# Graph attention on one core: a prologue written out chunk by chunk, and the adjacency turned into a bias by another engine

## The chip, the cores and the metric

One core of a Trainium2 chip runs the whole kernel. The metric is the device time of one execution in microseconds, the median over several runs. TensorE (PE) multiplies matrices, VectorE (DVE) and ScalarE (ACT) read its results out of PSUM, GpSimd (POOL) works in SBUF only, and SyncE (SP) issues DMAs. POOL and SP each issue DMAs into a queue of their own.

## The reference

Cut to what matters (N = 4096 rows, 256 features, 8 heads of 64):

```
h = max(layernorm(x), 0)
adj = max(adjacency, eye)
q, k, v = h @ Wq[head], h @ Wk[head], h @ Wv[head]
scores = q @ k.T / 8 + 0.01 * eye - 1e16 * (1 - adj)
out = x + sum over heads of softmax(scores) @ v @ Wo[head]
```

The adjacency is a float 4096 x 4096 matrix of zeros and ones.

## The kernel before, in words

The eight heads go in two groups of four. Each group has its own programs for the five engines, written one after the other: a prologue that makes keys K2 (a high and a low part, for accuracy) and values V for all 4096 rows, and then 64 steps, one for each head of each pair of row tiles (16 pairs of 256 query rows, four heads). The two groups are called group 0 and group 1 below. The order of work of each engine is written by hand, with semaphores between the engines.

**Prologue.** The rows go in NC = 8 chunks of 512. In group 0, DVE takes the statistics of a chunk of x (`bn_stats`, L647, L650, L652), POOL raises the variance to the power -0.5 (L319), DVE normalises (L658), PE transposes (L393), ACT takes the maximum with zero into `hc` and writes it to a DRAM scratch hT (L557, L560). Group 1 reads hT back (L178) from SP's queue. Then PE makes keys (L407) and values (L422), ACT and DVE read them out of PSUM (L566, L671 for keys, L572, L677 for values). The chunks run in a loop with two buffers, each chunk's values right behind its keys. After the last chunk, PE makes the first head's score slots (L449) with nothing between them.

**A step.** A score row of 4096 columns is cut in SPT = 4 slots of 1024; a step has SLOTS = 8 slots (two row tiles q = 0, 1, four slots k each). For slot j, PE makes the scores into `psS[j % 2]` (L449) and DVE's `mask` adds the bias tile B and takes the row maximum in one instruction (L702). ACT takes the exponential (L589). For the last 16 of the 32 key tiles ("late" ones) DVE transposes blocks of 32 x 32 (L723, twice a step, once for each q) and 32 DMAs of 64 KB put the blocks in place, 16 issued by SP (L248) and 16 by POOL (L307), eight for each q. PE transposes the other key tiles (L462, ACT copies them out, L596) and multiplies with V (L472, and L486 for the late tiles). The masks run one head ahead: step h masks slots 2 to 7 of head h+1 and slots 0 and 1 of head h+2. `mask` of slots 4 to 7 writes where the late blocks of the head before were staged, so it waits for the moves of that head: slots 4, 5 for the two halves of q = 0, slots 6, 7 for those of q = 1. L623 is ACT's copy of the odd half of a step's output, the last instruction of a step on ACT; its start is taken as the end of the step.

**The bias.** B holds (adj - 1) * 1e16 * 8 in bf16 for one pair of row tiles, for all four heads. In group 0, POOL loads it from the adjacency with a cast (L287, eight DMAs a pair) and turns it into the bias itself (`convert`, L293, eight a pair); the diagonal is cleared with `notI` (L298) in the one slot `own_slot` that holds the pair's own columns. The own slot is 0 for pairs 0 to 3, 1 for pairs 4 to 7, 2 for 8 to 11, 3 for 12 to 15. Group 0 also stores the finished bias to DRAM (`keep_bias`), and group 1 loads it back from SP's queue (L184) with no conversion. For pair i+1 this is done in steps h = 2 and h = 3 of pair i, when the last head's masks free B slot by slot. POOL's order in step 2 is: moves of q = 0, loads 0 and 1, moves of q = 1, loads 2 and 3, the base rows (L310), then

```
for half_ in range(2):
    for k in (2 * half_, 2 * half_ + 1):
        convert(i + 1, 0, k, own_slot)
    for k in (2 * half_, 2 * half_ + 1):
        load_adj(i + 1, 1, k)
for k in range(2):
    convert(i + 1, 1, k, own_slot)
```

and in step 3 the moves of both q, then the last two conversions.

Of the kernel before, what the change touches and what calls it, by code (L numbers as in the profile page):

```python
# [6 lines left out]
ACT = mybir.ActivationFunctionType  # L7
# [31 lines left out]
NC = N // CH  # L39
EPS = 1e-5  # L40
# [41 lines left out]
def group_programs(nc, sem, g, before, x, hT, adj, bias, Wk, Wq, Wv, Wo, base, result, t):  # L82
# [5 lines left out]
    (K2, V, S, B, PT, QH, QL, hq, wq, wo, O, Oodd, RB, acc, res, ident, notI, diag, mx, negm, sums, den, rden,  # L88
# [8 lines left out]
    x_in = [sem(f"x_in{g}{b}") for b in range(2)]  # L97
    h_in = [sem(f"h_in{g}{b}") for b in range(2)]
    h_out = [sem(f"h_out{g}{b}") for b in range(2)]
    (w_in, wqo_in, half_set, stat1, aggr, var_ready, rstd_ready, normed, x_transposed, h_ready, k_proj, v_proj, k_hi, k_lo,  # L100
     v_act, v_dve) = (sem(f"{s}{g}") for s in (
         "w_in", "wqo_in", "half_set", "stat1", "aggr", "var_ready", "rstd_ready", "normed", "x_transposed", "h_ready",
# [9 lines left out]
    (bias_conv, bias_ready, q_proj, q_hi, q_lo, scores_ready, slot_masked, row_ready, probs_ready,  # L112
# [3 lines left out]
            "bias_conv", "bias_ready", "q_proj", "q_hi", "q_lo", "scores_ready", "slot_masked", "row_ready",  # L116
# [3 lines left out]

    def chunks(engine, body):

        with engine.Fori(0, NC // 2 - 1) as i:
            for b in range(2):
                body(i, b, True, True)
        body(NC // 2 - 1, 0, True, False)
        body(NC // 2 - 1, 1, False, False)

    def after(i, b):

        return (i, 1) if b == 0 else (i + 1, 0)

    def query_psum(first):

        return psT[0] if first else psP
# [31 lines left out]
    if not norm:  # L167
        late_used_before, late_moved_before, late_sent_before, slot_masked_before, projected_before, o_summed_before, head_added_before, bias_kept_before = before

    def sync_program(sp):  # L170
# [3 lines left out]
        def load_x(i, b):  # L174
            sp.dma_start(xb[b], x_v[bass.ds(i * 2 + b, 1), :, :, :].rearrange("a p r d -> p (a r) d")).then_inc(x_in[b], 16)

        def load_h(i, b):
            sp.dma_start(hc[b], hT[:, :, bass.ds((i * 2 + b) * CH, CH)]).then_inc(h_in[b], 16)  # L178


# [16 lines left out]
        load = load_x if norm else load_h  # L197
        if not norm:
            sp.wait_ge(late_used_before, STEPS - 1)
        load(0, 0)  # L200
        if not norm:
            for q in range(QT):
                for half in range(HALVES):
                    sp.wait_ge(late_moved_before[q][half], MOVED * STEPS)
                    sp.wait_ge(late_sent_before[q][half], MOVED * STEPS)
        for w, dst in ((Wk, wk), (Wv, wv)):
            for c in range(DC):
                sp.dma_start(dst[:, c, :].rearrange("p (h k) -> p h k", k=KD),
                             w[heads, c * P:(c + 1) * P, :].rearrange("h p k -> p h k")).then_inc(w_in, 16)
        load(0, 1)  # L210
        if not norm:
            sp.wait_ge(projected_before, STEPS + START)
        for c in range(DC):
            sp.dma_start(wq[:, c, :].rearrange("p (h k) -> p h k", k=KD),
                         Wq[heads, c * P:(c + 1) * P, :].rearrange("h p k -> p h k")).then_inc(wqo_in, 16)
        Wo_v = Wo[heads, :, :].rearrange("(a e) k d -> e k a d", e=2)
        for e in range(2):
            sp.dma_start(wo[e * KD:(e + 1) * KD, :, :], Wo_v[e]).then_inc(wqo_in, 16)
        if not norm:
# [5 lines left out]
        with sp.Fori(0, NC // 2 - 1) as i:  # L225
            for b in range(2):
                if norm:
                    sp.wait_ge(x_transposed, i * 2 + b + 1)
                else:
                    sp.wait_ge(v_proj, i * 4 + (2 * b + 2 + START))  # L230
                load(i + 1, b)


        if norm:
            sp.wait_ge(h_out[0], 16 * (1 + START))
        load_hq(0)
        if norm:
            for b in range(2):
                sp.wait_ge(h_out[b], 16 * (NC // 2 + START))
# [39 lines left out]
    def gpsimd_program(pool):  # L279
# [9 lines left out]
        def convert(i, q, k, own_slot):  # L289

            wait_apart(pool, adj_in[q][k], i * 16 + 16, pool_passed)
            part = B[:, q, k * SLOT:(k + 1) * SLOT]
            done = nc.gpsimd.tensor_scalar(part, part, -1.0, MASK_VAL / SCALE, ALU.add, ALU.mult)  # L293
            if k == own_slot:
                done.then_inc(bias_conv, 1)
                pool.wait_ge(bias_conv, i * QT + q + 1)
                own = B[:, q, bass.ds(i * QW + q * P, P)]
                done = nc.gpsimd.tensor_tensor(own, own, notI[:, :], ALU.mult)  # L298
            done.then_inc(bias_ready, 1)
# [16 lines left out]
        def inverse_deviation(i, b):  # L316

            pool.wait_ge(var_ready, i * 2 + (b + 1))
            nc.gpsimd.tensor_tensor(rstd[:, b, :], mv[:, b, :, 1], half[:, :], ALU.pow).then_inc(rstd_ready, 1)  # L319

# [594 lines left out]
```

## Time and profile before

| what | value |
|---|---|
| median of 3 runs | 2713.36 us (2710.54 to 2719.93) |
| the profiled execution's own time | 2709.6 us |
| its span, first to last instruction | 2708.1 us |
| mean granted TensorE clock | 0.994 |
| busy share: PE, DVE, ACT, POOL | 97%, 83%, 68%, 47% |
| first score matmul of group 0, of group 1 | 85.51 us, 1439.23 us |
| first PE transpose of step 0, group 0 and group 1 | 101.10 us, 1454.64 us |

A row of a timeline has start and duration in us, the engine, the line of the kernel, the operation, output<-inputs, the shape and the number of instructions merged (x); in brackets stands how long the engine sat idle before it, and what released it. A row of a waits view has the waiting instruction, what it waited for, the total in us, how many times, and the longest. A row of a windows view has the stretch, its length, and busy time of each engine with instruction counts, then the granted clock, the share of the DMA engines that was busy, and GB/s. A row on one instruction has min/median/max of its duration in ns. PE counts as busy while a matmul is in its pipeline.

### The profile page before, as it was taken

The page shows a single profiled execution, that of the slowest core. Times are in us where ns is not written, and L with a number is a line of the kernel's source. Part 1 is how long each engine was busy: PE and PEld are TensorE (multiplying, and loading weights), DVE is VectorE, ACT ScalarE, POOL GpSimd, SP SyncE. Part 2 cuts the span into 40 slices and gives each one's busy share as a digit, 9 for nine tenths or more (in the row PEclk, how much of TensorE's full clock was granted, in tenths as well). Part 3 has the DMA queues.
Part 4 walks back from the last instruction along what each step waited for, and adds up shares of the span by engine and source line. Part 5 has one row for each costly group of instructions (what it writes and reads, how often), then busy time and mean ns, then how long its engine had stood idle before and what let it go on. Part 6 is the DMA issues. An engine that isn't in the chain of part 4 may idle for free. (4 is left out here: it accounts for less than half of the span.)

```text
span 2708.1 us, 58752 instructions
## 1 busy us (share of the span) xinstructions
PE 2630.7 (97%) x17344; PEld 1901.9 (70%) x17344; DVE 2253.6 (83%) x3833; ACT 1850.8 (68%) x3041; POOL 1280.6 (47%) x2418
## 2 busy tenths in 40 slices
PE   7899999999999999999998999999999999999997
PEld 5666777767777776766766777777777777777775
DVE  6788888888888888888847888888888888888885
ACT  3576777767767676776745777777777777777774
POOL 2356655566565556655512444444444444343433
PEclk9999999999999999999999999999999999999999
DMA  6367766677776677776652566656565656555654
GB/s 163 111 143 177 184 163 175 165 168 167 173 190 170 164 177 166 171 171 169 167 142 76 146 158 151 158 142 145 138 151 145 164 146 162 133 146 138 157 144 106
DMA packets 263358, 418.51 MB, mean 155 GB/s; under 512 B 98944, under 2 KB 119936, under 8 KB 259200
## 3 DMA queue, kind: packets, MB, share of 16 engines
q1 hardware_dynamic: 172032, 228.88, 33.0%
q0 software_dynamic: 89088, 184.69, 29.7%
q10 hardware_dynamic: 2176, 4.19, 0.4%
q8 instruction: 28, 0.46, 0.1%
q14 instruction: 34, 0.28, 0.0%
HBM read 136.31 MB, written 46.27 MB: 67 GB/s over the span
## 5 line engine op out<-in xcount | busy, mean ns | idle before, releaser
L307 POOL DMA_DIRECT2D S<-S x2048 | 1007.8, 500 | 1137.1 <-DVE S L723 1089.6
L702 DVE CUSTOM_DVE_ANT_0 S<-psS,B 128x1024 f32<-128x1024 f32 x1024 | 1228.4, 1218 | 268.3 <-PE psS L449 155.1
L589 ACT ACTIVATE S<-S,negm 128x1024 f32<-128x1024 f32 (+1 forms) x768 | 1095.8, 1428 | 88.8 <-DVE negm L709 88.3
L596 ACT ACTIVATE PT<-psT 128x512 f32<-128x512 f32 x1024 | 595.0, 596 | 267.5 <-PE psT L462 248.5
L449 PE MATMUL psS<-K,QH 128*128 128x512 f32 x2048 | 729.2, 437 | 35.7 <-DVE mx L702 31.5
L449 PE MATMUL psS<-K,QL 128*128 128x512 f32 x2048 | 642.5, 395 | 0.0
L462 PEld LDWEIGHTS psT<-ident,S 128*128 128x128 f32 x4096 | 481.2, 140 | 192.0 <-issue 73.5
L462 PE MATMUL psT<-ident,S 128*128 128x128 f32 x4096 | 608.0, 276 | 7.8 <-ACT S L589 4.9
L723 DVE STREAM_TRANSPOSE S<-S 128x2048 f32<-128x2048 f32 x256 | 590.2, 2306 | 27.6 <-PE psO L486 23.7
L472 PE MATMUL psO<-PT,V 128*64 128x256 f32 x4096 | 492.1, 382 | 0.0
L486 PE MATMUL psO<-S,V 128*64 128x256 f32 x4096 | 470.3, 382 | 2.0 <-DMA S<-S 2.0
L449 PEld LDWEIGHTS psS<-K,QL 128*128 128x128 f32 x2048 | 385.3, 188 | 87.4
L486 PEld LDWEIGHTS psO<-S,V 128*64 128x64 f32 x4096 | 283.6, 137 | 176.5 <-issue 48.0
L472 PEld LDWEIGHTS psO<-PT,V 128*64 128x64 f32 x4096 | 283.4, 137 | 175.0 <-ACT PT L596 23.7
L449 PEld LDWEIGHTS psS<-K,QH 128*128 128x128 f32 x2048 | 313.6, 191 | 82.0 <-DVE mx L702 69.6
L623 ACT ACTIVATE Oodd<-psO 64x256 f32<-64x256 f32 x128 | 48.9, 382 | 400.7 <-PE psO L472 400.7
L293 POOL TENSOR_SCALAR B<-B 128x1024 bf16<-128x1024 bf16 x128 | 133.4, 1052 | 59.6 <-DMA B<-in_adj 58.4
L589 ACT ACTIVATION_READ_ACCUMULATOR S<-S,negm 128x1 f32 x768 | 146.0, 190 | 0.0
L685 DVE TENSOR_TENSOR QL<-psP,QH 64x256 fp32r<-64x256 f32 x248 | 104.4, 421 | 3.6
L708 DVE TENSOR_TENSOR S<-S,diag 128x128 f32 (+1 forms) x256 | 75.2, 294 | 30.9 <-DVE mx L702 23.3
L580 ACT ACTIVATE QH<-psP 64x256 fp32r<-64x256 f32 x248 | 93.1, 375 | 2.2
L702 DVE DVE_READ_ACCUMULATOR2_ANT mx<- 128x1 f32 x1024 | 84.9, 83 | 0.0
(51 smaller groups left out, 967.9 us busy)
## 6 DMA issues: line engine op xcount, KB each, us to landing
S<-S SPq DMA_DIRECT2D x2048, 64.0 KB, 3.1
S<-S POOLq DMA_DIRECT2D x2048, 64.0 KB, 2.9
B<-in_adj POOLq DMA_DIRECT2D x128, 256.0 KB, 7.2
bias_scratch<-B SPq DMA_DIRECT2D x32, 1024.0 KB, 5.8
B<-bias_scratch SPq DMA_DIRECT2D x128, 256.0 KB, 5.1
hq<-hT_scratch SPq DMA_DIRECT2D x32, 256.0 KB, 3.5
RB<-rden_scratch SPq DMA_DIRECT2D x128, 64.0 KB, 3.2
S<-in_x SPq DMA_DIRECT2D x8, 512.0 KB, 3.6
```

The costliest lines, as they stand in the source:

```text
L293: done = nc.gpsimd.tensor_scalar(part, part, -1.0, MASK_VAL / SCALE, ALU.add, ALU.mult)
L307: pool.dma_start(dst, src).then_inc(late_sent[q][half], 16)
L449: last = nc.tensor.matmul(psS[j % 2][:, b * BANK:(b + 1) * BANK], part[:, h, q * P:(q + 1) * P], K2[:, h, col:col + BANK], start=hi, stop= ...
L462: last = nc.tensor.transpose(psT[s % 2][:, a * QW + q * P:a * QW + (q + 1) * P], S[:, h % 2, q, col:col + P], ident[:, :])
L472: last = nc.tensor.matmul(psO[a * KD:(a + 1) * KD, 0:QW], V[:, 2 * s + a, h * KD:(h + 1) * KD], PT[:, s % RING, a * QW:(a + 1) * QW], star ...
L486: last = nc.tensor.matmul(psO[half_ * KD:(half_ + 1) * KD, 0:QW], V[:, MT - LATE + m, h * KD:(h + 1) * KD], PTL[:, m, :, :, :], start=Fals ...
L580: last = nc.scalar.activation(QH[half_ * KD:(half_ + 1) * KD, h + e, :], query_psum(first)[e * KD:(e + 1) * KD, 0:QW], ACT.Copy)
L589: nc.scalar.activation(part, part, ACT.Exp, bias=negm[:, h % 2, q:q + 1], accum_out=sums[:, h % 2, q, e:e + 1]).then_inc(probs_ready, 1)
L596: nc.scalar.activation(PT[:, s % RING, :], psT[s % 2][:, :], ACT.Copy).then_inc(pt_act, 1)
L685: last = nc.vector.tensor_tensor(QL[rows, h + e, :], query_psum(first)[e * KD:(e + 1) * KD, 0:QW], QH.bitcast(F32)[rows, h + e, :], ALU.su ...
L702: nc.vector.tensor_tensor_reduce(out=part, in0=psS[j % 2][:, :], in1=B[:, q, k * SLOT:(k + 1) * SLOT], scale=SCALE, scalar=LOWEST, op0=ALU ...
L723: nc.vector.transpose(dst, src).then_inc(late_transposed, 1)
```

## The change

- **Prologue, written out.** Instead of a loop over two buffers there are four x buffers (XB = 4) and a buffer of `hc` for every chunk (chunks 0 to 3 in S of even heads, 4 to 7 in S of odd heads). PE makes keys of all chunks in order; values of chunks 0 to 3 (EARLY = 4) go between the keys, one chunk behind; values of chunks 4 to 7 go amid the first head's score slots, one chunk behind each two slots. wv moves into a buffer of PT. The first query goes to `psP` and is made after the keys of chunk 6. The normalisation goes from DVE to POOL, the stores of hT from ACT's queue to SP's.
- **Group 1's start.** SP issues the loads of h chunks 0 to 3, wq and hq first, then Wk, then Wv, then chunks 4 to 7. Group 0's last projection is made by PE behind the keys of group 1's chunk 0.
- **The bias.** POOL no longer converts. `add_self` clears the diagonal of the adjacency block (`notI`) and adds the identity (`eye`), two instructions of 128 columns. DVE converts each slot right before it masks it, in place, and waits for its own conversion.

```diff
-        def convert(i, q, k, own_slot):
-            wait_apart(pool, adj_in[q][k], i * 16 + 16, pool_passed)
-            part = B[:, q, k * SLOT:(k + 1) * SLOT]
-            done = nc.gpsimd.tensor_scalar(part, part, -1.0, MASK_VAL / SCALE, ALU.add, ALU.mult)
...
+        def add_self(i, q, own_slot):
+            wait_apart(pool, adj_in[q][own_slot], i * 16 + 16, pool_passed)
+            own = B[:, q, bass.ds(i * QW + q * P, P)]
+            nc.gpsimd.tensor_tensor(own, own, notI[:, :], ALU.mult).then_inc(self_cleared, 1)
+            wait_apart(pool, self_cleared, i * QT + (q + 1), pool_passed)
+            nc.gpsimd.tensor_tensor(own, own, eye[:, :], ALU.add).then_inc(self_added, 1)
...
         def step(i, h, more, prev, own_slot):
             move_late(i, h, 0)
-            if adj_step:
-                for k in range(2):
-                    load_adj(i + 1, 0, k)
+            if adj_rest:
+                add_self(i + 1, 1, own_slot)
             move_late(i, h, 1)
...
+            if adj_step:
+                for k in range(SPT):
+                    load_adj(i + 1, 0, k)
             if prev and h == 2:
                 pool.wait_ge(stored, i * 16)
                 load_base(i)
             if adj_step:
...
+                add_self(i + 1, 0, own_slot)
+                for k in range(SPT):
+                    load_adj(i + 1, 1, k)
...
         def mask(i, h, j, first=False):
             if h == 0 and norm:
+                dve.wait_ge(self_added, i * QT + (q + 1))
+                wait_apart(dve, adj_in[q][k], i * 16 + 16, dve_passed)
+                part = B[:, q, k * SLOT:(k + 1) * SLOT]
+                nc.vector.tensor_scalar(part, part, -1.0, MASK_VAL / SCALE, ALU.add, ALU.mult).then_inc(bias_ready, 1)
                 dve.wait_ge(bias_ready, i * SLOTS + (j + 1))
...
         def rows_again():
             sp.wait_ge(late_used_before, STEPS - 1)
+            for n in range(EARLY):
+                load_h(n)
+            load_weights(Wq, wq, wq_in)
+            load_hq(0)
             for q in range(QT):
                 for half in range(HALVES):
                     sp.wait_ge(late_moved_before[q][half], MOVED * STEPS)
                     sp.wait_ge(late_sent_before[q][half], MOVED * STEPS)
+            load_weights(Wk, wk, w_in)
+            sp.wait_ge(late_used_before, STEPS)
+            sp.wait_ge(pt_free_before, RING + STEPS * TS)
+            load_weights(Wv, wv, wv_in)
+            for n in range(EARLY, NC):
+                load_h(n)
...
+        def normalise(n):
+            pool.wait_ge(var_ready, n + 1)
+            b = n % XB
             nc.gpsimd.tensor_tensor(rstd[:, b, :], mv[:, b, :, 1], half[:, :], ALU.pow).then_inc(rstd_ready, 1)
+            pool.wait_ge(rstd_ready, n + 1)
+            for r in range(CR):
+                last = nc.gpsimd.tensor_scalar(xb[b][:, r, :], xb[b][:, r, :], mv[:, b, r, 0:1], rstd[:, b, r:r + 1],
+                                               ALU.subtract, ALU.mult)
+            last.then_inc(normed, 1)
...
+        for n in range(NC):
+            keys(n)
+            if n == 0 and not norm:
+                project_before(pe)
+            if norm and n + 2 < NC:
+                transpose_x(n + 2)
+            if 0 < n <= EARLY:
+                value_rows(n - 1)
+            if n == NC - 2:
+                query(0, 0, True, True)
+        pe.wait_ge(k_lo, NC * GROUP)
+        for n in range(SLOTS // 2):
+            scores(0, 0, 2 * n, True)
+            scores(0, 0, 2 * n + 1, True)
+            value_rows(EARLY + n)
         scores(0, 1, 0)
         scores(0, 1, 1)
```

## Rows read from the trace of the kernel before

**Rows 1.** The page: busy time, share and instructions of each engine.
```profile
PE 2630.7 (97%) x17344; PEld 1901.9 (70%) x17344; DVE 2253.6 (83%) x3833; ACT 1850.8 (68%) x3041; POOL 1280.6 (47%) x2418
```

**Rows 2.** Windows: steps 1 to 63 of group 0, then of group 1.
```profile
125.00:1376.00 1251.00, 1224.31 (x8264) 884.69 (x8262) 1049.11 (x1763) 873.62 (x1433) 717.57 (x1300) 1.00 0.71 169
1479.00:2693.00 1214.00, 1208.73 (x8266) 884.55 (x8264) 1047.35 (x1764) 871.27 (x1432) 513.57 (x1031) 1.00 0.60 148
```

**Rows 3.** Timeline of ACT: ends of steps 1, 2, 3, one pair.
```profile
705.87 0.38 ACT L623 ACTIVATE Oodd<-psO 64x256 f32<-64x256 f32 x1 [2.96 <-PE psO L472]
...
727.11 0.38 ACT L623 ACTIVATE Oodd<-psO 64x256 f32<-64x256 f32 x1 [2.77 <-PE psO L472]
...
746.64 0.38 ACT L623 ACTIVATE Oodd<-psO 64x256 f32<-64x256 f32 x1 [2.85 <-PE psO L472]
```

**Rows 4.** Waits of the masks for moves, group 0 and then group 1.
```profile
DVE S L702 <- DMA S<-S: 57.0, 56, 2.6
...
DVE S L702 <- DMA S<-S: 16.7, 18, 1.5
```

**Rows 5.** Timeline of POOL in the same two steps.
```profile
706.42 1.19 POOL L287 DMA_DIRECT2D B<-in_adj  x2
...
711.68 1.10 POOL L287 DMA_DIRECT2D B<-in_adj  x2
...
719.23 1.04 POOL L293 TENSOR_SCALAR B<-B 128x1024 bf16<-128x1024 bf16 x1 [2.35 <-DMA B<-in_adj]
...
721.79 1.05 POOL L293 TENSOR_SCALAR B<-B 128x1024 bf16<-128x1024 bf16 x1 [0.92 <-DMA B<-in_adj]
722.78 1.13 POOL L287 DMA_DIRECT2D B<-in_adj  x2
...
725.94 7.90 POOL L307 DMA_DIRECT2D S<-S  x16
```

**Rows 6.** All adjacency loads (L287): issue to landing.
```profile
DMA to landing us min/median/max: 4.5/7.2/16.2
```

**Rows 7.** Single instructions: DVE tensor_scalar twice, POOL's diagonal clearing.
```profile
L658 DVE TENSOR_SCALAR S<-S,mv,rstd x32: 395/406/1126, 8.1 to 70.8; 128x256 f32<-128x256 f32 x32
...
L652 DVE TENSOR_SCALAR mv<-mv x8: 169/170/171, 6.7 to 65.9; 128x4 f32<-128x4 f32 x8
...
L298 POOL TENSOR_TENSOR B<-B,notI x32: 422/430/543, 68.2 to 1295.5; 128x128 bf16 x28, 128x128 bf16<-128x128 bf16 x4
```

**Rows 8.** Timeline of DVE in step 3: masks of slots 2, 5, 7.
```profile
728.69 1.23 DVE L702 CUSTOM_DVE_ANT_0 S<-psS,B 128x1024 f32<-128x1024 f32 x1 [0.89 <-PE psS L449]
...
735.28 1.23 DVE L702 CUSTOM_DVE_ANT_0 S<-psS,B 128x1024 f32<-128x1024 f32 x1 [1.09 <-DMA S<-S]
...
738.77 1.23 DVE L702 CUSTOM_DVE_ANT_0 S<-psS,B 128x1024 f32<-128x1024 f32 x1
```

**Rows 9.** Timeline of PE in group 0's prologue.
```profile
12.95 6.50 PE L407 MATMUL psS<-S 128*128 128x512 f32 x8 [1.26 <-ACT S L557]
...
59.61 3.60 PE L407 MATMUL psS<-S 128*128 128x512 f32 x8
...
63.92 1.89 PE L422 MATMUL psO<-S 128*128 128x256 f32 x8
...
67.38 3.60 PE L407 MATMUL psS<-S 128*128 128x512 f32 x8
...
85.51 0.70 PE L449 MATMUL psS<-K,QH 128*128 128x512 f32 x2 [1.22 <-DVE QL L685]
...
101.10 1.11 PE L462 MATMUL psT<-ident,S 128*128 128x128 f32 x4 [2.46 <-ACT S L589]
```

**Rows 10.** Timeline around the start of group 1.
```profile
1372.99 0.83 SPq L178 DMA_DIRECT2D S<-hT_scratch  x1
...
1380.09 5.39 PE L407 MATMUL psS<-S 128*128 128x512 f32 x8 [1.71 <-DMA S<-in_Wv]
...
1454.64 0.65 PE L462 MATMUL psT<-ident,S 128*128 128x128 f32 x4 [2.46 <-ACT S L589]
```

More of the change, by code:

```diff
@@ L119, in group_programs @@
             "rden_stored", "rden_in"))
[L121 to L135, printed above, removed]
     def wait_taken(engine, i, h, s):
@@ L167, in group_programs, with project @@
     if not norm:
-        late_used_before, late_moved_before, late_sent_before, slot_masked_before, projected_before, o_summed_before, head_added_before, bias_kept_before = before
+        late_used_before, late_moved_before, late_sent_before, slot_masked_before, projected_before, o_summed_before, head_added_before, bias_kept_before, pt_free_before, project_before = before
+    def project(pe, i, h):
+        pe.wait_ge(o_ready, count(i, h, 1, 1 + START))
+        pe.wait_ge(head_added, count(i, h, 1, START - 1))
+        for q in range(QT):
+            last = nc.tensor.matmul(psP[:, q * D:(q + 1) * D], O[:, q * P:(q + 1) * P], wo[:, h // 2, :], start=True, stop=True)
+        last.then_inc(projected, 2)
     def sync_program(sp):
@@ L224, in sync_program @@
                     load_bias(0, q, k)
[L225 to L231, printed above, removed]
-        if norm:
[L235 to L239, printed above, removed]
+        if norm:
+            first_rows()
+        else:
+            rows_again()
         sp.sem_inc(rden_stored, 16 * START)
@@ L489, in values_late @@
                 last.then_inc(late_used, 1)
-        def project(i, h):
-            pe.wait_ge(o_ready, count(i, h, 1, 1 + START))
-            pe.wait_ge(head_added, count(i, h, 1, START - 1))
-            for q in range(QT):
-                last = nc.tensor.matmul(psP[:, q * D:(q + 1) * D], O[:, q * P:(q + 1) * P], wo[:, h // 2, :], start=True, stop=True)
-            last.then_inc(projected, 2)
         def step(i, h, nxt, nxt2, prev):
@@ new lines, in scalar_program @@
+            relu(1)
+        for n in range(NC):
+            keys_hi(n)
+            if norm and n + 2 < NC:
+                relu(n + 2)
+            if 0 < n <= EARLY:
+                value_rows(n - 1)
+            if n == NC - 2:
+                query_hi(0, 0)
+        act.sem_inc(pt_act, PT_START)
+        value_rows(EARLY)
+        value_rows(EARLY + 1)
+        exps(0, 0, 0, 0)
+        exps(0, 0, 0, 1)
+        value_rows(EARLY + 2)
+        exps(0, 0, 0, 2)
+        value_rows(EARLY + 3)
@@ L781, in step @@
                 transpose_late(i1, h1, 1, True)
-        dve.sem_inc(k_lo, 2 * GROUP)
-        dve.sem_inc(v_dve, START)
         if norm:
             nc.vector.memset(half[:, :], -0.5).then_inc(half_set, 1)
-            statistics(0, 0)
-            normalise(0, 0)
-            statistics(0, 1)
-        chunks(dve, keys_values)
+            for n in range(XB):
+                statistics(n)
+        for n in range(NC):
+            keys_lo(n)
+            if norm and n + XB < NC:
+                statistics(n + XB)
+            if 0 < n <= EARLY:
+                value_rows(n - 1)
+            if n == NC - 2:
+                for e in range(2):
+                    query_lo(0, 0, e)
         dve.sem_inc(head_added, START)
@@ L797, in vector_program @@
         if norm:
[L798 to L804 removed]
+            dve.wait_ge(consts, 4)
+            for b in range(XB):
+                dve.wait_ge(h_out[b], 16 * (NC // XB))
+        for n in range(SLOTS // 2):
+            mask(0, 0, 2 * n, first=True)
+            mask(0, 0, 2 * n + 1, first=True)
+            if n == 2:
+                transpose_late(0, 0, 0, False)
+            value_rows(EARLY + n)
         mask(0, 1, 0)
         mask(0, 1, 1)
+        transpose_late(0, 0, 1, False)
         steps(dve, step)
```

300 lines of the change are left out of this document (132 added, 168 removed).

## The prediction

> **What bounds the kernel now.** I read the page first, for the engines' shares. PE is at 97% and DVE at 83% [rows 1], so a step costs what PE needs unless something holds PE up. The windows view shows where something does. The 63 steps of group 0 take 1251 us and those of group 1 take 1214 us, with nearly the same PE busy time (1224.31 and 1208.73) and the same DVE busy time [rows 2]. So group 0 loses about 37 us, 26.7 of it as idle PE, and POOL is the engine whose work differs (718 against 514 us). That is the most that a free bias could bring. The ends of steps show where it lies: step 2 of a pair takes 727.11 - 705.87 = 21.2 us and step 3 takes 19.5 us [rows 3], against a mean of 19.3 in group 1 [rows 2]. The waits view gives the mechanism: masks wait for moves of late blocks 57.0 us in group 0 and 16.7 in group 1 [rows 4]. In step 2 POOL puts two loads (1.19 us) ahead of the moves of q = 1 [rows 5], and slots 6 and 7 wait for those moves. Outside the steps there are two prologues: 101.10 us until step 0 of group 0 starts [rows 9], and from 1380.09 to 1454.64 for group 1, which stands idle for its weights first [rows 10]. Both end with ten score slots and a wait of 2.46 us for the exponential.
>
> **Prologue of group 0.** PE's work stays the same, only its order changes. A chunk with values takes 67.38 - 59.61 = 7.77 us, its values 3.46, its keys with transposes 4.31 [rows 9]. After the change the first keys come later, because PE transposes two chunks first and POOL's normalisation of the second is done only at about 13.7 (a power of 1 us and four tensor_scalars of 0.5 for each chunk, by POOL's 0.43 for 128 columns [rows 7]). I take 15.5 in place of 12.95. Then: first keys 6.5 as before, transposes 0.9, four chunks of 7.77, one of 4.3, two of 3.5 with a query of 0.9, and about 2 us until the last keys have been read out (1.22 of waiting shows at this place although a query and values lie ahead of it [rows 9]). That is 68.2. The ten slots took 101.10 - 85.51 - 2.46 = 13.1 us. PE now has values between them, so DVE's masks are covered, and I take 11.5. Four values of 3.46 make 13.8. Step 0 starts at 93.5, and the 2.46 goes, because the exponentials now lie beside the last values. Gain 7.6 us (6 if slots keep 13.1; 10 if the keys start at 12.95).
>
> **Prologue of group 1.** Here a cost is hidden in SP's order. SP is free at 1372.99, behind the last step's own DMAs [rows 10]. Before, one h load and then the weights were issued, and keys began at 1380.09. After the change four h loads (0.83 us to issue and 512 KB each), wq and hq stand ahead of Wk in the same queue. The data ahead of Wk grows by 1.5 MB for h alone; at the 240 GB/s that 169 GB/s at a DMA share of 0.71 stand for [rows 2] this is 6.5 us (an estimate), less some 2 us because keys no longer wait for Wv as well. So keys begin at about 1384.3, 4.2 later. From there: keys 5.4 at the clock of that start, projection 1.1, seven chunks of keys 24.5, four values 13.8, query 0.9, read-out 2, slots and values 25.3: 73.0, so 1457.3 against 1454.64. Loss 2.7 us (gain 3 if Wk lands as early as before, loss 5 if it lands last).
>
> **First steps.** They last 23 us each from the first PE transpose. I give each 1 us for the filled gap ahead of it. DVE's second block transpose now stands behind two masks of the next head and is late there, which is why it isn't more. Gain 2 (bounds: gain 6, loss 2).
>
> **Step 2, fifteen times.** POOL issues the moves of q = 1 before any load, 1.19 us earlier, and no load data is ahead of them. Slots 6 and 7 stop waiting. I take 1.1 us a step, 16.5 in all; the lower bound is 8, the upper 25.
>
> **Step 3, the conversions.** Six of a pair's eight conversions are in step 3, two at the end of step 2 where DVE still reaches slot 2 with 0.89 us to spare [rows 8]. The trace has no such instruction on DVE. From below, its fixed part alone is 0.17 us (four columns). From above, a tensor_scalar of 256 f32 columns takes 0.406, so 1024 columns take 0.17 + 4 x 0.236 = 1.11 us [rows 7]. The row above is nearest in kind, but it reads f32 and two operands per partition where the new one reads bf16 and constants, so I take 0.5, with 0.15 for DVE's wait on itself: 0.65 a slot. Slot 2 absorbs its own. Slots 3 to 7 add 5 x 0.65 = 3.25, less the 1.09 that slot 5 waits for moves anyway [rows 8]: 2.2 us later at slot 7, and the step ends 746.64 - 738.77 = 7.9 us behind slot 7's mask [rows 3, 8]. For eleven pairs this is 24 us (bounds 6 to 57).
>
> The row says 0.92 ns a column for the f32 tensor_scalar [rows 7]. The Trainium skill, page "VectorE: DVE Perf Modes", section on the perf-mode tier table, gives this operation four columns a cycle for bf16 in SBUF and two for f32. The f32 row here shows one, so trace and page differ on the neighbour; by the page's 693 ns for 2048 columns the conversion would take 0.43 us, a slot 0.58, and the sum would come out 4 us lower.
>
> **Step 3, the held queue.** `add_self` waits on POOL for the load that holds the pair's own columns, and behind it stand the loads of q = 1 (in step 2) and the moves of q = 1 (in step 3). This is cheap when the own slot is early and dear when it is slot 3. Worked out on the pair of the rows: loads of q = 0 are issued from 710.5. In the rows the third and fourth load land at 719.2 and 721.6, 7.5 and 9.4 us behind their issue [rows 5]; over the whole prologue batch of eight the last lands 16.2 behind its issue [rows 6]. So the first of a batch takes about 6 and each further one about 1.8. The fourth lands at 722.4, the diagonal (two operations of 0.43 and two waits, 1.3 us [rows 7]) is done at 723.7. Only then are the loads of q = 1 issued, in place of 715.8 and 722.8; the fourth lands at about 735.1, the diagonal is done at 736.4, and the eight moves of q = 1 go out until 740.4, where they ended at 725.94 + 7.90 = 733.8 [rows 5]. They land 2 us later, 742.4, and slot 7 needs them. With step 2 shorter by 1.1, step 3 begins at 726.0: slot 7 at 16.4 in place of 11.7 us into the step. That is 4.7 to 5 us for each of the four pairs with own slot 3, 20 us, conversions included because they hide in the wait. For own slots 0 to 2 the same chain ends before slot 7 is reached by DVE. Bounds: 0 if loads land 4 us sooner, 45 if slot 2 suffers as well.
>
> **Sum.** -7.6 + 2.7 - 2 - 16.5 + 24 + 20 = +20.6 us on the profiled execution's 2709.6, so 2730. That execution lies 3.8 below the median, so 2734 as a median. A measurement of this kernel can tell about 0.3% (8 us).
>
> **Rivals.**
> - No change (0.18): the conversion costs little more than its fixed part, 0.32 a slot with the wait. Then eleven pairs lose 6 in place of 24: 2716. For it: DVE is idle 202 of 1251 us in group 0 [rows 2] and the 128 conversions need 41. Against it: DVE's idle time is small around slots 3 to 7.
> - Faster (0.20): the fourth adjacency load lands before DVE's block transpose of q = 0 is done, some 4 us sooner than in my chain, so POOL is never held, and the conversion is cheap. Then only the 6 us stand against the gains: -7.6 + 2.7 - 2 - 16.5 + 6 = -17, so 2696, and 2688 with the better bound of group 0's prologue. It decides at a landing within 6 us in all. For it: the shortest landing is 4.5 [rows 6]. Against it: 1.8 us a load behind the first.
> - Conversion at one column a cycle (0.16): 1.26 a slot, 5 x 1.26 - 1.09 = 5.2, times eleven 57, and 24 for the others: 2709.6 + 58, as a median 2771. For it: the f32 row. Against it: half the bytes.
> - My forecast, 0.46, its own range 2722 to 2752.
>
> So slower by over 0.3% 0.62, within 0.3% 0.18, faster 0.20. The range 2694 to 2762 leaves out the far half of the fast case and most of the slow one.
>
> **What the profile would show.** First score of group 0 near 68 and first step at 93.5; first keys of group 1 at 1384 (counted from the last step's end: 8.4 us of idle PE). DVE's TENSOR_SCALAR of 1024 bf16 columns at 0.5 us. Step 2 at 20.2, step 3 at 21.7 for the first eleven pairs and 24.5 for the last four, with waits of masks on the diagonal or on moves there. Group 1's steps unchanged. I am wrong if group 0's steps come out shorter than 1251 us, if step 3 doesn't depend on the own slot, or if the conversion shows 1.1 us.

## The result, and the profile after

The changed kernel takes 2752.67 us (median of four runs, 2751.14 to 2756.2), the kernel before 2715.39 on the same chip. The ratio is 1.0138, with a 95% interval of 1.0124 to 1.0153. So it is 37 us slower. The prediction said 2734 us, 19 above this 2715.39; the measured time lies inside its range (2694 to 2762). Medians of one kernel differ from chip to chip by up to 0.8% (the kernel before showed 2706, 2715, 2725 and 2727), so kernels of different chips are compared below by their ratio to the kernel before, and steps by the trace.

The page after. The first fence holds the engines' busy times, which answer to [rows 1]. POOL has lost 81 us of busy time and DVE has gained 33.

```profile
PE 2639.7 (96%) x17344; PEld 1908.1 (69%) x17344; DVE 2286.8 (83%) x3929; ACT 1853.1 (67%) x3041; POOL 1199.6 (44%) x2356
```

The windows view of the changed kernel has one row for the 63 steps of group 0, one for the stretch between the groups and one for the 63 steps of group 1 (start and end, length, busy time of each engine, granted clock, DMA share, GB/s). It answers to [rows 2].

```profile
122.20:1417.60 1295.40, 1239.78 (x8268) 890.53 (x8268) 1092.00 (x1884) 876.88 (x1433) 607.01 (x1211) 0.99 0.69 164
1417.60:1522.40 104.80, 90.78 (x374) 61.90 (x374) 63.85 (x101) 47.25 (x80) 12.44 (x25) 0.92 0.35 102
1522.40:2734.90 1212.50, 1208.88 (x8268) 884.99 (x8267) 1048.32 (x1764) 871.41 (x1434) 512.39 (x1032) 1.00 0.60 148
```

The whole loss lies in group 0's steps: 1295.4 in place of 1251.6 us. The start up to the end of step 0 is 2.1 us shorter, the stretch between the groups (102.7 before) 2.0 longer, and group 1's steps are 2.2 shorter. Sorted by their place in the pair (ends of steps, as in [rows 3]), group 0's steps average, before and after: step 0 20.21 and 20.21, step 1 18.88 and 19.11, step 2 21.26 and 20.04, step 3 19.13 and 22.87. Step 2 gained 19.5 us over its sixteen times, step 3 lost 60.

The waits view of group 0's steps in the changed kernel (us in total, times, longest) answers to [rows 4]:

```profile
POOL B L309 <- DMA B<-in_adj: 103.6, 27, 7.7
...
DVE S L720 <- DMA S<-S: 37.5, 39, 2.4
DVE S L720 <- DVE B L710: 28.1, 97, 0.8
...
DVE B L710 <- POOL B L311: 11.5, 8, 2.1
```

The masks (L720) wait less for moves than before, 37.5 us against 57.0. In their place stands a wait for DVE's own conversion (L710), and POOL's self-loop step (L309) waits 104 us for the own slot's load, with the rest of POOL's queue behind it. The last line is DVE's conversion waiting for the self-loop step itself: all eight waits lie in the four pairs with own slot 3, at slot 0 in step 2 and at slot 4 in step 3.

The timeline of DVE in one step 3 (the ninth pair's, which begins at 823.1 us) shows conversions and masks of slots 2 to 7, to be held against [rows 8]:

```profile
823.95 0.38 DVE L710 TENSOR_SCALAR B<-B 128x1024 bf16<-128x1024 bf16 x1
824.72 1.22 DVE L720 CUSTOM_DVE_ANT_0 S<-psS,B 128x1024 f32<-128x1024 f32 x1 [0.39 <-PE psS L462]
...
826.56 1.23 DVE L720 CUSTOM_DVE_ANT_0 S<-psS,B 128x1024 f32<-128x1024 f32 x1 [0.27 <-DVE B L710]
...
831.09 1.23 DVE L720 CUSTOM_DVE_ANT_0 S<-psS,B 128x1024 f32<-128x1024 f32 x1 [1.66 <-DMA S<-S]
...
833.16 1.23 DVE L720 CUSTOM_DVE_ANT_0 S<-psS,B 128x1024 f32<-128x1024 f32 x1 [0.50 <-DMA S<-S]
...
836.09 1.23 DVE L720 CUSTOM_DVE_ANT_0 S<-psS,B 128x1024 f32<-128x1024 f32 x1 [0.28 <-DVE B L710]
...
837.95 1.23 DVE L720 CUSTOM_DVE_ANT_0 S<-psS,B 128x1024 f32<-128x1024 f32 x1 [0.28 <-DVE B L710]
```

Two things are to be seen. Slots that wait for nothing else are 1.85 us apart (0.42 of conversion, 0.28 of waiting for it, 1.15 of mask), where a mask directly behind another needs 1.15. And slot 4 starts 8.0 us into the step, behind a wait of 1.66 us for the moves of q = 0, so slot 7 starts at 14.8 (837.95 - 823.13). In the pair of [rows 8] slot 7 started 738.77 - 727.11 = 11.7 us into its step. Meanwhile POOL did this (its timeline, the same pair, end of step 2 and start of step 3):

```profile
808.12 2.50 POOL L303 DMA_DIRECT2D B<-in_adj  x4
...
816.33 0.42 POOL L309 TENSOR_TENSOR B<-B,notI 128x128 bf16 x1 [4.81 <-DMA B<-in_adj]
...
817.60 2.39 POOL L303 DMA_DIRECT2D B<-in_adj  x4 [0.23 <-issue]
820.13 3.94 POOL L319 DMA_DIRECT2D S<-S  x8
826.82 0.42 POOL L309 TENSOR_TENSOR B<-B,notI 128x128 bf16 x1 [2.74 <-DMA B<-in_adj]
...
828.04 3.95 POOL L319 DMA_DIRECT2D S<-S  x8 [0.19 <-issue]
```

The first self-loop step holds the loads of q = 1 until 817.6, and they go out in one burst directly ahead of the moves. The second holds the moves of q = 1 until 828.0. In the run these two suspects, and the conversion, can't be told apart, so they were taken away one by one.

### The profile page after: what moved, and what is told of

Same layout as the page of the kernel before. It is cut to its first block and busy times, and to the rows that moved or that the text cites. A ratio compares the mean times of both kernels' runs of the same rounds, so it can differ in the third digit from the quotient of the medians.

```text
span 2749.6 us, 58455 instructions
## 1 busy us (share of the span) xinstructions
PE 2639.7 (96%) x17344; PEld 1908.1 (69%) x17344; DVE 2286.8 (83%) x3929; ACT 1853.1 (67%) x3041; POOL 1199.6 (44%) x2356
## 5 line engine op out<-in xcount | busy, mean ns | idle before, releaser
L720 DVE CUSTOM_DVE_ANT_0 S<-psS,B 128x1024 f32<-128x1024 f32 x1024 | 1231.0, 1219 | 249.7 <-PE psS L462 129.1
L720 DVE DVE_READ_ACCUMULATOR2_ANT mx<- 128x1 f32 x1024 | 85.1, 83 | 0.0
L303 POOL DMA_DIRECT2D B<-in_adj x128 | 70.3, 551 | 14.2 <-DVE mx L720 3.3
```

What stands on the lines that cost most here:

```text
L720: nc.vector.tensor_tensor_reduce(out=part, in0=psS[j % 2][:, :], in1=B[:, q, k * SLOT:(k + 1) * SLOT], scale=SCALE, scalar=LOWEST, op0=ALU ...
```

## The experiments

### The bias path put back: does the prologue cost anything?

The changed kernel, with POOL's step and DVE's mask as before.

```diff
-                add_self(i + 1, 0, own_slot)      # and DVE's tensor_scalar in mask()
+            # before's order of load_adj, move_late and convert
```

> The changed kernel's prologue with the bias path of the kernel before: POOL subtracts, multiplies and clears its own diagonal, slot by slot, and the loads of the first two slots stand ahead of the second row's moves again. If the bias path carries the whole loss (theory A), the 63 steps of the first group go back to some 1252 us and the time to 2705 to 2716, within 0.3% of the kernel before, since the prologues and the second group came out at -2, +2 and -2 us. If the loss comes from the written-out prologue or from where the tiles now lie (theory B), the steps keep most of their 44 us and the time stays above 2740.

Measured: ratio 0.9999 (0.9974 to 1.0025), 2723.9 us. Group 0's steps take 1258.0 us, step 3 19.1. So the bias path carries the loss, and the written-out prologues are worth nothing that this timing can tell (its interval is 7 us either way). In the trace step 0 of group 0 does end 4.9 us sooner than before (119.4 against 124.3), but the stretch between the groups is 1.5 us longer and the steps 6.3. Theory B falls.

### One cause away, the other away, both away

The first kernel has no self-loop step (`add_self` and the wait for it), the second no conversion (DVE's `tensor_scalar`), the third neither. Without a conversion, SP's store of the bias waits for the masks instead.

```diff
-                dve.wait_ge(self_added, i * QT + (q + 1))           # first, third; add_self() gone too
-                nc.vector.tensor_scalar(part, part, -1.0, ...)       # second, third
-            sp.wait_ge(bias_ready, i * SLOTS + SLOTS)              # second, third: keep_bias
+            sp.wait_ge(slot_masked, count(i, 0, SLOTS, SLOTS))
```

> The changed kernel without the self-loop step on POOL and without VectorE's wait for it (left out: the self connection in the mask, so the diagonal keeps what the adjacency says). VectorE still converts. Theory 'held queue' (POOL's queue and the moves behind it wait for the own slot's load; the prediction's +20): step 3 falls from 22.9 to about 21.5 and the time to about 2730. Theory 'conversion' (the slots are 0.65 us further apart, whatever POOL does): step 3 stays above 22.3 and the time above 2742.

> The changed kernel without VectorE's conversion (left out: the mask's bias is the raw 0 or 1); POOL's self-loop step, the loads and the waits for them stay. Theory 'conversion': the slots of step 3 go back from 1.85 to some 1.2 us apart, step 3 falls to about 19.5 and the time by 45 to 55 us, to 2697 to 2707. Theory 'held queue': step 3 falls by the priced 2.2 us only, to about 20.7, and the time by some 25 us, to about 2725.

> The changed kernel with neither the self-loop step nor the conversion (both left out, so the mask is wrong): only the loads, their order and the waits for their landing are left. If the two causes add, the time is that of the changed kernel less both single savings. If the landing of the loads and of the moves behind them sets the second row's slots by itself (theory C), step 3 stays above 20.5 and the time is not under 2715. Conversion and held queue as the only causes give step 3 at 18.5 to 19.1 and a time of about 2690.

Measured on one chip, with the average of 14 middle pairs for the start of slots 4 and 7 in step 3, and for its length:

| kernel | ratio to before (interval) | steps of group 0, us | slot 4 at | slot 7 at | step 3 |
|---|---|---|---|---|---|
| before (first chip) | 1 | 1251.6 | 6.4 | 11.6 | 19.4 |
| changed (first chip) | 1.0138 (1.0124 to 1.0153) | 1295.4 | 8.4 | 15.3 | 23.6 |
| no self-loop step | 1.0037 (1.0023 to 1.0050) | 1274.1 | 6.8 | 13.4 | 21.6 |
| no conversion | 1.0061 (1.0038 to 1.0083) | 1286.7 | 8.1 | 14.3 | 22.3 |
| neither | 0.9880 (0.9861 to 0.9900) | 1236.7 | 5.9 | 11.0 | 18.9 |

Neither theory's numbers came in for both single runs: without the self-loop step the step fell about as the held queue forecast, without the conversion it fell less than either theory said. By the changed kernel's ratio on the first chip each saving alone is small (1.0% and 0.8%), and both together give 2.6%: the two causes overlap. Either of them alone makes step 3 longer than with neither, by 2.7 us (conversion) and 3.3 us (self-loop step), and both make 4.7. The run with neither also shows that the loads, their new order and their landing cost nothing (theory C falls); with both costs gone the reordered queue is 1.2% faster than before. In the run without conversion DVE's timeline names what is left (the ninth pair's step 3, slot 4 and slot 5):

```profile
824.53 1.23 DVE L717 CUSTOM_DVE_ANT_0 S<-psS,B 128x1024 f32<-128x1024 f32 x1 [2.43 <-DMA S<-S]
...
826.66 1.23 DVE L717 CUSTOM_DVE_ANT_0 S<-psS,B 128x1024 f32<-128x1024 f32 x1 [0.90 <-DMA S<-S]
```

Slots 4 and 5 wait for moves of q = 0, which no self-loop step stands ahead of in step 3. Their landing explains it: on average SP's moves of q = 0 are issued from -2.6 us (counted from the step's start) and the last lands at 9.2, with loads of q = 1 issued from -5.8; with neither cause the moves are issued from -2.2 and land by 7.1, with loads issued from -11.6 on, one by one. POOL's land at 9.1 against 5.1, issued from -2.9 against -4.2. So the four held loads issued just ahead of the moves make them late; the run with the loads first, below, bears this out. Whether their lateness or their going out in one burst does it, no run separates.

### Which of the two self-loop steps holds what

The first self-loop step holds the loads of q = 1 (the first hold), the second the moves of q = 1 (the second hold). The first kernel here issues the loads of q = 1 ahead of the first self-loop step. The second keeps the changed kernel's order there and puts the second self-loop step behind the moves of q = 1.

```diff
             if adj_step:
-                add_self(i + 1, 0, own_slot)
                 for k in range(SPT):
                     load_adj(i + 1, 1, k)
+                add_self(i + 1, 0, own_slot)
...
-            if adj_rest:                       # the other kernel
-                add_self(i + 1, 1, own_slot)
             move_late(i, h, 1)
+            if adj_rest:
+                add_self(i + 1, 1, own_slot)
```

> The changed kernel with one call moved: in step 2, POOL issues the second row's four loads first and does the first row's self-loop step after them. The two places where the self-loop step holds POOL's queue are told apart. Theory 'first hold' (the loads held until the end of step 2 land amid the moves of step 3 and slow them): the loads are issued at -11.6 to -7.0 us as in the run without a self-loop step, the first row's moves land by 6 instead of 8 us, step 3 falls from 23.6 to about 21.6 and the ratio to the kernel before from 1.0138 to about 1.004 (2735). Theory 'second hold' (the second row's moves wait behind the second self-loop step): step 3 stays above 22.8 and the ratio above 1.010.

> The changed kernel with the second self-loop step behind the second row's moves on POOL in step 3; the first one stays ahead of the second row's loads. Theory 'first hold' (from the run with the loads first, which took 31 to 35 us off the first group's steps): nothing is gained, since the loads stay late; slot 4 then waits for the self-loop step itself, which ends some 4 us later, so step 3 is 23.3 to 25 and the ratio 1.012 to 1.022. Theory 'second hold': the second row's moves land 3 us sooner, step 3 falls by 1 us or more and the ratio to 1.008 or less.

The changed kernel was run again on the chip of the second one:

> The changed kernel as it is, on the chip of the next two runs, so that they can be compared with it and not only with the kernel before. Ratio to the kernel before again 1.011 to 1.016, step 3 of the first group at 23.6 us and its last slot at 15.3 us.

Measured: loads first, ratio 1.0066 (1.0044 to 1.0089); group 0's steps 1260.2 us in place of 1295.4, step 3 21.4. The changed kernel again: 1.0097 (1.0075 to 1.0120), which is lower than forecast and than on the first chip; its steps of group 0 take 1300.3 us, slot 7 starts at 15.4, step 3 takes 23.4. Second self-loop step behind the moves: 1.0126 (1.0107 to 1.0145), steps 1302.8, slot 7 at 15.2, step 3 23.2. POOL in the run with the loads first, the same pair:

```profile
792.05 1.14 POOL L303 DMA_DIRECT2D B<-in_adj  x2
795.50 0.53 POOL L303 DMA_DIRECT2D B<-in_adj  x1 [2.31 <-DVE mx L720]
796.68 0.53 POOL L303 DMA_DIRECT2D B<-in_adj  x1 [0.66 <-DVE mx L720]
797.23 0.44 POOL L309 TENSOR_TENSOR B<-B,notI 128x128 bf16 x1
797.85 0.43 POOL L311 TENSOR_TENSOR B<-B,eye 128x128 bf16 x1 [0.18 <-POOL B L309]
799.31 4.06 POOL L319 DMA_DIRECT2D S<-S  x8 [1.03 <-DVE S L741]
803.39 0.44 POOL L309 TENSOR_TENSOR B<-B,notI 128x128 bf16 x1
```

The own slot has landed by the time that POOL comes to it, twice, so both holds are gone by this one edit. The loads are issued from -11.5 us, and the last moves of q = 0 land at 4.9 (POOL) and 6.4 us (SP), where the changed kernel has 9.3 and 9.1. The step now costs as much as without any self-loop step (21.4 and 21.6). So the first hold, with what follows from it, is the held queue's price: 2.0 to 2.2 us of step 3 against the changed kernel's two traces, some 30 us over fifteen pairs. The ratios give less: 0.7% or 20 us against the changed kernel's 1.0138, and 0.3% against the 1.0097 of its second run, where the intervals overlap. Why they give less is open.

The second hold is not priced at zero by the run that moves it. There slot 4's conversion waits in every pair for the self-loop step, which now comes later (0.5 to 1.5 us), so one wait was put in the place of another, as the expectation of the first hold's theory had it. In the four pairs with own slot 3, step 3 does fall, to 23.2 us from 24.6 in the changed kernel on this chip, but slot 2 starts 1.1 us sooner there already, ahead of the second hold; in the other eleven it is 23.2 against 22.7. That the moves of q = 1 don't bind is seen in the changed kernel's own trace: over the 14 middle pairs the last of them lands at 13.1 us on average, slot 7 starts at 15.3, and in 13 of the 14 it waited for nothing but its conversion, in the last for PE.

### What a conversion's price is made of

On top of the loads-first kernel, one conversion for two slots.

```diff
-                part = B[:, q, k * SLOT:(k + 1) * SLOT]
+                if j % 2 == 0:
+                    part = B[:, q, k * SLOT:(k + 2) * SLOT]
```

> As the run with the loads first, but VectorE converts two slots with one instruction (2048 columns) ahead of each even slot and nothing ahead of the odd one. If a slot's price is 0.41 us of conversion and 0.3 us of waiting for its own write, a pair costs 0.8 + 0.3 instead of 1.4 us: the last slot of step 3 starts some 0.9 us sooner and the time is about 13 us under that of the run with the loads first (ratio 0.999). If the price is the columns alone, or the second slot's load is what is waited for, the gain is under 4 us.

Measured: ratio 0.9967 (0.9955 to 0.9980) against 1.0066 for the loads-first kernel on the same chip; slot 7 starts at 12.4 in place of 13.5 us; group 0's steps take 1243.7. A view of all the conversions in the paired kernel, and DVE's timeline of one pair of slots in step 3:

```profile
L712 DVE TENSOR_SCALAR B<-B x64: 649/694/927, 73.8 to 1282.9; 128x2048 bf16<-128x2048 bf16 x64
```

```profile
797.82 0.69 DVE L712 TENSOR_SCALAR B<-B 128x2048 bf16<-128x2048 bf16 x1
798.80 1.23 DVE L722 CUSTOM_DVE_ANT_0 S<-psS,B 128x1024 f32<-128x1024 f32 x1 [0.29 <-DVE B L712]
...
799.95 1.22 DVE L722 CUSTOM_DVE_ANT_0 S<-psS,B 128x1024 f32<-128x1024 f32 x1
```

Two slots cost 0.69 + 0.29 = 0.98 us in place of 2 x 0.70 = 1.40. Slot 7's start, 1.1 us sooner, is near the 0.9 of the first theory, so the wait of an instruction for DVE's own last result is as much a part of the price as the columns are. The time fell by twice what was forecast, 27 us by the medians in place of 13. The two traces, 22.7 us apart, have 16.5 of it in group 0's steps, 2.7 ahead of them (the first head's slots are converted too) and 4.3 in group 1's steps, where nothing was changed. This kernel alone already beats the kernel before.

### A version that beats both

POOL converts again, so DVE's slots are free, but the queue keeps the order that the change gave it (moves of q = 1 ahead of all loads), and no conversion stands ahead of a load or a move that is due. The cut below is against the kernel before.

```diff
             move_late(i, h, 0)
+            if adj_rest:
+                convert(i + 1, 1, 0, own_slot); convert(i + 1, 1, 1, own_slot)
             move_late(i, h, 1)
             if adj_step:
-                for k in range(2): load_adj(i + 1, 0, k)        # and conversions amid the loads
+                for k in range(SPT): load_adj(i + 1, 0, k)
+                load_adj(i + 1, 1, 0); load_adj(i + 1, 1, 1)
+                convert(i + 1, 0, 0, own_slot)
+                load_adj(i + 1, 1, 2)
+                convert(i + 1, 0, 1, own_slot)
+                load_adj(i + 1, 1, 3)
+                convert(i + 1, 0, 2, own_slot); convert(i + 1, 0, 3, own_slot)
+            if adj_rest:
+                convert(i + 1, 1, 2, own_slot); convert(i + 1, 1, 3, own_slot)
```

> The changed kernel's prologue and its place of the moves (the second row's ahead of the first loads), but POOL converts: in step 2 all eight loads, with the first row's four conversions between and behind the last of them; in step 3 two conversions between the two rows' moves and two behind them. If step 2's gain (20.0 instead of 21.3) is that of the order alone and step 3's loss that of the conversion and the held queue alone, step 2 takes 20.1 and step 3 about 19.0, as in the run without both, and the ratio is about 0.991 (2700). If the four conversions in a row hold step 3's first moves, or the second row's hold its slots, step 3 is above 20.3 and the ratio 0.998 or more.

Measured: ratio 0.9919 (0.9901 to 0.9937), 2684.0 us. Step 2 averages 20.0, step 3 19.1 in the 14 middle pairs, and the windows view of group 0's steps gives 1225.3 us:

```profile
119.40:1344.70 1225.30, 1213.31 (x8268) 886.14 (x8268) 1063.38 (x1764) 872.60 (x1434) 716.17 (x1301) 1.00 0.71 173
```

POOL is as busy as before the change (716 against 718 us) and group 0 is 26 us shorter in this trace, so POOL's order and not its amount of work was what cost that time. The trace is of the fastest execution, 6.5 us under the median; the next two kernels, whose bias path is the same, show 1238.7 and 1244.2 us for group 0's steps. What holds in all three is step 2, 20.0 to 20.1 us in place of 21.3, or 19 to 20 us over its sixteen times. Two further kernels take up the prologues. In the first VectorE normalises the first two chunks, and group 1's weights of the keys are loaded behind the first chunk; in the second VectorE normalises four.

```diff
+                if n < 2:                          # DVE; n < XB in the second kernel
+                    tensor_scalar(xb[n][:, r, :], ..., ALU.subtract, ALU.mult)
...
-            for n in range(EARLY): load_h(n)
-            load_weights(Wq, wq, wq_in); load_hq(0)
+            load_h(0)
             # waits for the moves of the last step
             load_weights(Wk, wk, w_in)
+            for n in range(1, EARLY): load_h(n)
+            load_weights(Wq, wq, wq_in); load_hq(0)
```

> The previous kernel with two more edits in the prologues. VectorE normalises the first two chunks of x, POOL the others: first keys at about 14 instead of 20.7 us and all of the first group's prologue some 6 us earlier, if the second chunk's normalisation on POOL (4.9 us) is what delays it; if the stream of chunks is bound elsewhere the gain is under 2 us. In the second group the weights of the keys are loaded behind the first chunk and ahead of the other three, wq and hq: the first keys begin about 5 us instead of 9.9 us behind the last step, and the gap between the groups falls by 4 to 5 us; if the keys then wait for the next chunks, by under 2 us. Together 10 us or 0.4% under the previous kernel, or none.

> As the kernel with both prologue edits, but VectorE normalises the first four chunks, POOL the other four. In that kernel the transposes of chunks 2 and 3 still waited 1.96 and 1.41 us for POOL. If POOL's 4.8 us a chunk is all that held them, the first score comes at 68 instead of 70.9 us and the time is about 3 us lower (ratio 0.987, hardly told from 0.988 by the timing, but plain in the trace). If VectorE then holds chunk 0's keys for the normalisations ahead of them, nothing is gained.

Measured: 0.9883 (0.9863 to 0.9902) and 0.9871 (0.9854 to 0.9887). PE's timeline of the first kernel, start of group 0 and start of group 1:

```profile
13.86 1.97 PE L419 MATMUL psT<-ident,S 128*128 128x128 f32 x8 [2.41 <-DVE S L823]
15.62 4.26 PE L434 MATMUL psS<-S 128*128 128x512 f32 x8
21.84 1.10 PE L419 MATMUL psT<-ident,S 128*128 128x128 f32 x8 [1.96 <-POOL S L343]
...
1355.17 3.70 PE L434 MATMUL psS<-S 128*128 128x512 f32 x8 [0.23 <-DMA S<-in_Wk]
```

The first keys come at 15.6 us. Of the 5.1 us gained there against the kernel without the prologue edits (20.69) 3.0 are left at the first score (70.90, from 73.93), because chunks 2 and 3 wait for POOL; with four chunks on VectorE the first score comes at 69.05. Group 1's keys begin 6.3 us behind the last issue for RB on SP, in place of 13.7, and the stretch between the groups takes 92.6 us in place of 103.6, more than the 4 to 5 forecast; 2.7 of these 11 stand in the last step instead, which took 16.9 us where it took 14.2 to 14.6 elsewhere. The second kernel's stretch takes 96.8 us, 6.9 less, with a last step of 14.4. The first kernel's median is 7.8 us under the kernel without the prologue edits, and the intervals of the two ratios just overlap. Its trace is only 1.3 us shorter, since the 14 us gained at the two places stand against group 0's steps, 13.4 us longer; no edit is known to do that.

## Why the prediction was right or wrong

The direction, the place and the two causes of the loss were right; its size and the path of one cause were not: +37 us measured, +19 forecast (the sum is +20.6, on the profiled execution of the kernel before). One reading at the start was wrong too: of the 37 us between the groups the prediction took 26.7 as idle PE, which is all of group 0's idle time; group 1 has 5.3 of its own [rows 2], so 21.4 is idle PE and 15.6 longer PE work. No term rests on it. By the steps of the prediction:

- **Step 2.** Forecast -16.5 (20.2 us a step). Measured 20.04 in place of 21.26, -19.5. Near.
- **The conversion's duration.** Forecast 0.5 us and 0.15 for the wait. The view of all of them has 0.42 (median of 128), and the wait is 0.28:

```profile
L710 DVE TENSOR_SCALAR B<-B x128: 379/421/500, 73.9 to 1338.6; 128x1024 bf16<-128x1024 bf16 x128
```

 The sum, 0.70, is near the 0.65 taken. The f32 row, the upper bound, was the wrong neighbour. The Trainium skill, page "VectorE: DVE Perf Modes", section on the perf-mode tier table, gives four columns a cycle for bf16; by the prediction's sentence on it the conversion takes 0.43 us, and the trace agrees (0.42, and 0.69 for 2048 columns in the paired kernel).
- **Step 3, the conversions.** Forecast 2.2 us a step. The run without the self-loop step shows the conversion alone: step 3 21.6 us against 19.4 before, 2.2. Right, though the other reading of the same run is that it takes 2.7 from a queue that would have given 18.9.
- **Step 3, the held queue.** This is the step that failed. The prediction had the last four pairs (own slot 3) at 24.5 and the first eleven at 21.7, "for own slots 0 to 2 the same chain ends before slot 7 is reached by DVE". Measured: 24.4 and 23.1. The other eleven are 1.4 us longer than forecast, 15 us in all. The chain that the prediction followed, through the second self-loop step and the moves of q = 1 to slot 7, is not the one that binds: those moves have landed before slot 7 is reached, in the last four pairs too (14.5 and 16.5 us into the step). Slot 4, not slot 7, waits. In the first eleven pairs it waits for the moves of q = 0. This goes through the first self-loop step: four loads issued from -5.8 us on the average in place of -11.6 on, the moves of q = 0 issued directly behind them and landed 2 to 4 us later. In the last four pairs DVE itself waits for the diagonal: in step 2 slot 0's conversion 0.7 to 1.8 us, so that slot 2 starts 1.4 us later than in the other pairs, and in step 3 slot 4's conversion 0.6 to 2.1 us, while the first moves of q = 0 land only then too (9.4 us into the step). There the prediction followed the chain to the diagonal, but not to who waits at its end, and that 24.5 came so near 24.4 is in part luck. A hold of loads was priced by who waits for the loads, and in most pairs nobody did; it had to be priced by what they then lie ahead of.
- **Prologue of group 0.** Forecast -7.6, and -1 for its first step. Measured -2.1 at the end of step 0. POOL's normalisation was priced at 0.5 us an instruction, from a 128-column row of another operation [rows 7]; it takes 1.22 us, three times VectorE's 0.406 for the same work:

```profile
L335 POOL TENSOR_SCALAR S<-S,mv,rstd x32: 1209/1219/1226, 8.1 to 56.1; 128x256 f32<-128x256 f32 x32
```

 That puts the first keys at 20.73 in place of 15.5. The read-out of the last keys took 3.24 us in place of 2, and behind it the granted clock was low: the windows view has 0.66 for 74.0 to 79.0 us, between its lower level (1.2 GHz) and its full one (2.4). The changed kernel's PE timeline shows score pairs of 0.98 to 1.05 us there, where 0.62 is the time at full clock, and values of 2.81 where 1.89 is.

```profile
73.95 0.73 PE L462 MATMUL psS<-K,QH 128*128 128x512 f32 x2 [3.24 <-DVE K L685]
...
74.98 0.98 PE L462 MATMUL psS<-K,QH 128*128 128x512 f32 x2
75.76 1.05 PE L462 MATMUL psS<-K,QL 128*128 128x512 f32 x2
76.62 2.81 PE L435 MATMUL psO<-PT,S 128*128 128x256 f32 x8
...
101.02 0.63 PE L475 MATMUL psT<-ident,S 128*128 128x128 f32 x4 [2.19 <-ACT S L604]
```

 And the last wait, for an exponential, stayed: 2.19 us at the first transpose of step 0, which starts at 101.02 as it did before [rows 9]. DVE's eight conversions amid the first slots keep it, which the prediction had at nothing here: in the run with POOL's bias path put back and in the one without conversion the wait is 0.45 us, the transpose comes at 99.3 and step 0 ends at 119.4 in place of 122.2, with the same prologue.
- **Prologue of group 1.** Forecast +2.7, and -1 for its first step, with keys beginning 8.4 us behind the last step. Measured +2.0 for both, with keys 9.9 behind it. That the two sums agree is luck: counted from the end of the last step of group 0, the first transpose comes 5.9 us later than before (84.7 against 78.7), and the first step is then 3.9 us shorter. SP's and PE's timelines show the order that the prediction named:

```profile
1414.98 2.69 SPq L172 DMA_DIRECT2D S<-hT_scratch  x4
...
1420.49 2.62 SPq L182 DMA_DIRECT2D S<-in_Wk  x2
```

```profile
1427.54 6.68 PE L416 MATMUL psS<-S 128*128 128x512 f32 x8 [9.93 <-DMA S<-in_Wk]
```

- **The rest.** Step 1 is 0.2 us longer, 4 us in all; it lies between 18.9 and 19.8 us in the other runs, whatever their bias path. Group 1's steps are 2 us shorter. No run was made for either.

Of 20.9 us by which the trace (+41.5 us of span) exceeds the forecast sum (+20.6), 15 are the first eleven pairs and 7 the prologues; step 2's 3 us against them, and step 1 and group 1, make the rest.

## What to carry to other kernels

When a wait is put into a queue, don't only ask who waits for the instructions behind it, ask what they will be next to when they are let go: here four held loads went out in one burst ahead of moves that were due, and cost some 2 us of each step 3, although in most pairs nobody waited for the loads themselves. When an instruction is moved to price its wait, look at who then waits for it: moving the second self-loop step only traded one wait for another. Two causes that overlap in one step have to be taken away together before either is judged, as each alone gave 1% or less here and both 2.6%. An operation that moves to another engine is priced from a row of that engine with the same kind of operands, and a conversion in a chain that sets the step is priced with the wait for its own result, which is saved by converting two tiles at once.

## What the runs showed of the hardware

- POOL needs 1.22 us for a subtract-and-multiply of 128x256 f32 with two operands per partition, DVE 0.406 [rows 7]; with constants POOL's 128x1024 bf16 takes 1.04 [rows 5]. So the number of columns alone prices nothing on POOL; whether the type or the operands make the difference, no run here shows.
- A bf16 tensor_scalar in place on DVE takes 0.42 us for 1024 columns and 0.69 for 2048, so 0.27 ns a column and 0.15 fixed, while the f32 form with operands per partition takes some 0.94 ns a column (0.406 us for 256 columns, with the 0.170 of 4 columns as its fixed part) [rows 7]. Whether the type or the operands make that difference, no run here shows.
- In some steps 3 of the changed kernel TensorE's granted clock falls. The windows view, for the ninth pair's step 3 and for the fourteenth's, gives 0.93 and 1.00, although PE was idle longer in the second (4.5 us against 3.0); what decides it is not shown. The full speed, 1.00, is the level of 2.4 GHz. The time behind slot 7's mask was 9.5 us in the first, against 7.9 on average in the kernel before. Over 14 pairs this came to 0.5 us a step in the first trace of the changed kernel and 0.1 in the second, so it isn't part of the steady cost.

```profile
823.10:847.40 24.30, 21.32 (x129) 14.09 (x129) 18.84 (x34) 13.65 (x21) 9.68 (x20) 0.93 0.74 156
1235.50:1260.00 24.50, 20.04 (x129) 13.51 (x129) 20.43 (x36) 13.70 (x22) 11.00 (x23) 1.00 0.66 150
```
